# Six layers of local attention and feed-forward issued as one stream on one Trainium2 core

## The reference, cut to what matters

```python
for i in range(6):
    x = attn_layer(shift_tokens(x), Wqkv[i], q_scale[i], k_scale[i], Wo[i]) + x
    x = ffn_layer(shift_tokens(x), ln_g[i], ln_b[i], W1[i], b1[i], W2[i], b2[i]) + x
# attn_layer: 16 heads of 64; q and k divided by their norms, scaled, rotated;
#   a softmax over a band of 33 keys; the heads' outputs times Wo
# ffn_layer: layer norm, xn @ W1 + b1 split in a and gate (341 each),
#   a * gelu(gate) @ W2 + b2
```

## Time and profile before, and how to read it

| | |
|---|---|
| median of three executions | 4304.59 us (4303.39 to 4310.63) |
| the profiled execution: its own time | 4307.25 us |
| its span, first to last instruction | 4305.4 us |
| mean granted TensorE clock | 0.974 of full speed |
| PE busy / PEld busy | 94% / 74% of the span |
| DVE / ACT / POOL busy | 84% / 71% / 70% |

### The profile page before, as it was taken

The page is one execution under the profiler, slowest core; times in us unless marked ns, Lnnn a source line. Parts: engine busy times, 40 slices in busy tenths (PEclk is TensorE's granted clock), DMA queues, the critical chain, the costliest instruction groups (busy, mean ns, idle before and its releaser), DMA issues.

```text
span 4305.4 us, 111689 instructions
## 1 busy us (share of the span) xinstructions
PE 4041.0 (94%) x30864; PEld 3177.6 (74%) x30864; DVE 3601.2 (84%) x12077; ACT 3057.7 (71%) x11197; POOL 3010.0 (70%) x3393
## 2 busy tenths in 40 slices
PE   7888887899998999989999999999899999999998
PEld 5777776688876888767888768887578886688875
DVE  5676665899978999968999789999699997899985
ACT  1455544788864888838888658888388885588883
POOL 2333332799965999928999659999299995699980
PEclk9999998999999999999999999999999999999998
DMA  4222221000000000000000000000000000000000
GB/s 146 80 79 79 79 85 56 6 0 0 0 21 7 1 0 0 0 21 7 0 0 0 21 7 1 0 0 0 26 1 0 0 0 21 7 0 0 0 0 20
DMA packets 75916, 82.96 MB, mean 19 GB/s; under 512 B 13622, under 2 KB 69396, under 8 KB 74836
## 3 DMA queue, kind: packets, MB, share of 16 engines
q1 hardware_dynamic: 75732, 80.87, 5.8%
HBM read 45.33 MB, written 35.52 MB: 19 GB/s over the span
## 4 chain that ended last, share of the span: by engine, by line
PE 79%; DVE 9%; issue 5%; ACT 4%; POOL 2%; DMA 0%; DVEq 0%; SPq 0%; POOLq 0%; ACTq 0%; PEldq 0%
PE bank_pair L981 11%; PE bank L992 10%; PE bank L1007 9%; PE bank L1015 8%; PE bank L456 8%; PE bank L972 7%; PE bank L458 6%; PE bank L457 6%; PE bank_pair L1203 2%; PE bank_pair L560 1%; PE bank L554 1%; PE bank L536 1%; DVE uf L1351 1%; ACT p L637 1%; ACT sc L626 1%
## 5 line engine op out<-in xcount | busy, mean ns | idle before, releaser
L1064 ACT ACTIVATE p<-p,mx 128x128 f32<-128x128 f32 x3072 | 1195.9, 403 | 46.9 <-DVE mx L1115 45.7
L1152 POOL TENSOR_TENSOR rot<-own_crossed 128x512 f32<-128x512 f32 x768 | 984.7, 1282 | 29.6 <-DVE own_crossed L1090 29.6
L1162 POOL TENSOR_TENSOR p<-p,ri 128x512 f32<-128x512 f32 x768 | 801.7, 1044 | 54.8 <-DVE ri L1112 54.0
L1146 POOL TENSOR_TENSOR rot<-rot,rn 128x512 f32<-128x512 f32 x768 | 803.7, 1046 | 0.0
L1115 DVE CUSTOM_DVE_ANT_0 p<-bank_pair,band_f 128x128 f32<-128x128 f32 x3072 | 692.1, 282 | 5.6
L1064 ACT ACTIVATION_READ_ACCUMULATOR p<-p,mx 128x1 f32 x3072 | 617.3, 201 | 0.0
L1122 DVE COPY pTl<-bank 128x512 f32<-128x512 f32 x768 | 530.3, 691 | 89.2 <-PE bank L1007 83.7
L456 PE MATMUL bank<-wqkv_hi,xs_lo 128*128 128x512 f32 x1152 | 563.4, 489 | 40.5 <-POOL xs_lo L1135 21.7
L1044 ACT ACTIVATE qkT<-bank 128x512 f32<-128x512 f32 x768 | 454.2, 591 | 173.9 <-PE bank L972 173.8
L981 PE MATMUL bank_pair<-qkT 64*128 64x128 f32 x6144 | 549.4, 297 | 3.8 <-DVE mx L1115 3.1
L992 PE MATMUL bank<-pTl,v_sb 128*64 128x128 f32 x6144 | 512.0, 288 | 24.6 <-DVE zS L1097 19.9
(11 more groups left out here) (195 smaller groups left out, 7253.1 us busy)
## 6 DMA issues: line engine op xcount, KB each, us to landing
pos_scratch<-pos_sb SPq DMA_DIRECT2D x32, 1020.0 KB, 4.3
sc<-pos_scratch SPq DMA_DIRECT2D x32, 512.0 KB, 4.0
own_crossed<-in_L_ffn_Wqkv SPq DMA_DIRECT2D x6, 1536.0 KB, 6.7
ctx_sb<-in_ctx SPq DMA_DIRECT2D x32, 128.0 KB, 3.5
wo<-in_L_ffn_Wo SPq DMA_DIRECT2D x6, 512.0 KB, 7.1
mrow<-in_mask_BxS_fk SPq DMA_DIRECT2D x1, 2048.0 KB, 7.7
x_all<-in_x SPq DMA_DIRECT2D x4, 512.0 KB, 8.7
out<-res SPq DMA_DIRECT2D x8, 256.0 KB, 2.3
```

The costliest lines, as they stand in the source:

```text
L1064: last = nc.scalar.activation(p[:, j, h, :], p[:, j, h, :], ACT.Exp, bias=mx[:, j, h:h + 1], scale=-1.0, accum_out=psums[:, j, h:h + 1])
L1146: nc.gpsimd.tensor_tensor(rot[:, j4, :, :], rot[:, j4, :, :], rn[:, jr, (k - 4) % 2, :].unsqueeze(2).to_broadcast([128, 2 * G, DL]), ALU.m ...
L1152: nc.gpsimd.tensor_tensor(rot[:, j4, :, :], own[:, j4, :, :], crossed[:, j4, :, :], ALU.add).then_inc(L["rot0"], 1)
L1162: nc.gpsimd.tensor_tensor(p[:, j, :, :], p[:, j, :, :], ri[:, j, :].unsqueeze(2).to_broadcast([128, G, T]), ALU.mult).then_inc(L["pn"], 1)
```

## The change: one stream over six layers

The four engines' attention and feed-forward functions are replaced by one function each (`stream_tensor`, `stream_scalar`, `stream_vector`, `stream_pool`), run by `stream`. Its body is sixteen iterations, four batches; in body q of a layer the units of quad q enter, and the feed-forward of quad q - 2 is put between them, piece by piece at the iterations `at.ffn(k)`. The bodies of all layers follow one another: the feed-forward of a layer's last two quads lies beside the attention of the next layer's first two. The skew of attention grows from 11 to 16 iterations, and the order of the pieces in an iteration is new. In detail:

- Feed-forward products all go through the bank of V (`ffn_ps = v_ps`, one bank); each of them, and each V, waits until the one before it in that bank has been copied or used.
- The mean is taken out by one product with `centre_w` (identity minus mean); the mean square comes by a product with `mean_w` on all 128 partitions at once. The root is exp(-0.5 ln), on ACT. The product with the root goes to POOL, with gain on ACT before it and the offset on ACT after it (twice: as float32 and rounded); the low part is POOL's.
- Gates: DVE copies them out of PSUM with the bias (`keep_gate`, three a quad, new); gelu then works in SBUF. Values are as before.
- ACT loads the gelu tables at iteration 9 and the Ln and Exp tables again at iteration 10: two loads a quad.
- Wqkv of the next layer is split in the first iterations of body 0 of that layer, six groups of 512 columns, each right after its old content has been used last; the high part by ACT, the low part by POOL. Its raw form has a buffer of its own. W1 is split by POOL at iteration 14 of body 1; biases, gains and rotary tables are renewed by small copies on ACT and DVE. SP waits for each weight by itself.

```diff
+        def stream(eng, emit):
+            def body(l, q):
+                for k in range(BODY):
+                    emit(l, q, k)
+            body(0, 0)
+            body(0, 1)
+            with eng.Fori(0, LAYERS - 1) as l:
+                with eng.Fori(2, QUADS) as q:
+                    body(l, q)
+                body(l + 1, 0)
+                body(l + 1, 1)
+            with eng.Fori(2, QUADS) as q:
+                body(LAYERS - 1, q)
+            body(LAYERS - 1, QUADS)
+            body(LAYERS - 1, QUADS + 1)
...
+            def next_layer(l):
+                wait_apart(sp, L["wqkv_split"], l * WEIGHT_GROUPS)
+                load_wqkv(l)
+                wait_apart(sp, L["tab"], l)
+                load_scales(l)
+                wait_apart(sp, Fm["w1_split"], l)
+                load_w1(l)
+                wait_apart(sp, Fm["gain"], l)
+                wait_apart(sp, Fm["bias"], l)
+                load_vecs(l)
+                wait_apart(sp, L["WO"], l * B)
+                load_wo(l)
+                wait_apart(sp, Fm["y_mm"], l * QUADS)
+                load_w2(l)
+            return first_attention, first_ffn, next_layer
...
+        def stream_tensor(pe):
+            SHARED_AHEAD_OF_FFN = {2: ("xcg", 1, 1), 6: ("rstd", 1, 1), 8: ("gate", 3, 2), 10: ("gate", 3, 3), 12: ("u", 3, 2), 14: ("u", 3, 3)}
+            SHARED_AHEAD_OF_V = {1: ("xcg", 1, 1), 3: ("rstd", 1, 1), 7: ("gate", 3, 2), 9: ("gate", 3, 3), 11: ("u", 3, 2), 13: ("u", 3, 3)}
...
+                def v_gone():
...
+                        pe.wait_ge(L["v"], at.P + (k - 8) // 2)
...
+                        pe.wait_ge(L["z"], QUADS + at.F)
...
+                        gone, each, done = SHARED_AHEAD_OF_FFN[k]
...
+                def gate(c):
...
+                def value(c):
...
+                if on(10):
...
                     last.then_inc(L["S"], 1)
+                if at.ffn(14):
...
+                    pe.wait_ge(Fm["w2_in"], 32 * (at.lf + 1))
+                    pe.wait_ge(Fm["u"], 3 * at.F + 3)
...
+                    last.then_inc(Fm["y_mm"], 1)
                 if on(9):
...
+                    last.then_inc(L["T1"], 1)
+                if at.ffn(6):
...
+                    pe.wait_ge(Fm["w1_split"], at.lf + 1)
+                    pe.wait_ge(Fm["xn"], at.F + 1)
+                    gate(0)
+                if at.ffn(10):
...
+                    value(0)
+                if on(15):
...
                     last.then_inc(L["PV"], 1)
+                if on(9) and k % 2 == 1:
+                    if at.ffn(15):
+                        pe.wait_ge(L["z"], QUADS + at.F + 1)
+                    elif at.ffn(1, 3, 7, 9, 11, 13):
+                        gone, each, done = SHARED_AHEAD_OF_V[k]
...
+                    if at.renew() and k in (9, 11):
+                        pe.wait_ge(L["wqkv_split"], l * WEIGHT_GROUPS + UB + (k - 9) // 2 + 1)
...
+                    split_product(v_ps[:, :], [x[:, (k - 9) // UB % 4, :] for x in xs], [w[:, 2, g * G * DL:(g + 2) * G * DL] for w in wqkv]).then_inc(L["proj"], 1)
+                if at.ffn(12):
...
+                    value(2)
+                if on(4):
...
+                    if at.renew() and 0 <= k - 4 < UB:
+                        pe.wait_ge(L["wqkv_split"], l * WEIGHT_GROUPS + (k - 4) + 1)
...
+                                  [w[:, 0:2, g * G * DL:(g + 1) * G * DL] for w in wqkv]).then_inc(L["proj_qk"], 1)
+                if at.ffn(6):
+                    pe.wait_ge(Fm["gate"], 3 * at.F + 1)
+                    gate(1)
+                if at.ffn(8):
...
+                    gate(2)
+                if on(13):
...
                     last.then_inc(L["T2"], 1)
+                if at.ffn(0):
...
+                    nc.tensor.matmul(ffn_ps.rearrange("p (a n) -> p a n", a=QUAD), centre_w[:, :], shifted(at.ffn_batch(), QUAD), start=True, stop=True).then_inc(Fm["centre"], 1)
+                if at.ffn(2):
...
+                    pe.wait_ge(Fm["xsq"], at.F + 1)
+                    nc.tensor.matmul(ffn_ps[:, :], mean_w[:, :], xsq[:, :], start=True, stop=True).then_inc(Fm["var"], 1)
+                if at.ffn(10):
+                    pe.wait_ge(Fm["u"], 3 * at.F + 1)
+                    value(1)
+                if on(15) and (k - 15) % UB == UB - 1:
...
                     last.then_inc(L["WO"], 1)
...
+        def stream_scalar(act):
+            def use_table(which):
+                act.add_instruction(mybir.InstLoadActFuncSet(act_func_set_id=which, name=nc.get_next_instruction_name(), engine=mybir.EngineType.Activation))
...
+                def gelu(c):
...
+                    nc.scalar.activation(gel[0:m, c, :], gel[0:m, c, :], ACT.Gelu).then_inc(Fm["gelu"], 1)
+                def round_group(e):
...
+                if on(9):
...
+                    nc.scalar.activation(qkT[:, (k - 9) % 2, :, :].rearrange("p c n -> p (c n)"), qkT_ps[:, :], ACT.Copy).then_inc(L["qkT"], 1)
+                if on(15):
...
+                    nc.scalar.activation(oT[:, (k - 15) % 8, :], oT_ps, ACT.Copy).then_inc(L["oT"], 1)
+                if at.ffn(10):
+                    gelu(1)
+                    gelu(2)
+                    use_table(LOG_EXP_SET)
+                if on(7) and k % 2 == 1:
...
                     nc.scalar.activation(ss_log[:, j, :, :], ssc[:, j, :, :], ACT.Ln, scale=ROOT_GAIN ** 2).then_inc(L["ss_log"], 1)
...
+                    nc.scalar.activation(rn[:, (k - 7) // 2 % 4, :, :], ss_log[:, j, :, :], ACT.Exp, scale=-0.5).then_inc(L["rn"], 1)
+                if on(9) and k % 2 == 1:
...
+                    nc.scalar.activation(v_sb[:, (k - 9) % 8:(k - 9) % 8 + 2, :, :].rearrange("p u h n -> p (u h n)"), v_ps[:, :], ACT.Copy).then_inc(L["v"], 1)
+                if at.renew() and k in (5, 7):
+                    round_group(UB + (k - 5) // 2)
+                if on(10):
...
                         last = nc.scalar.activation(p[:, j, h, :], p[:, j, h, :], ACT.Exp, bias=mx[:, j, h:h + 1], scale=-1.0, accum_out=psums[:, j, h:h + 1])
...
+                if at.ffn(0):
+                    act.wait_ge(Fm["centre"], at.F + 1)
...
+                    nc.scalar.activation(xsq[:, :], ffn_ps[:, :], ACT.Square).then_inc(Fm["xsq"], 1)
+                    nc.scalar.activation(xcg[:, :], ffn_ps[:, :], ACT.Copy, scale=gain[:, 0:1]).then_inc(Fm["xcg"], 1)
+                if at.ffn(2):
...
+                    nc.scalar.activation(rstd[:, :], ffn_ps[:, :], ACT.Ln, bias=eps_col[:, 0:1], scale=1.0).then_inc(Fm["log"], 1)
...
+                    nc.scalar.activation(rstd[:, :], rstd[:, :], ACT.Exp, scale=-0.5).then_inc(Fm["rstd"], 1)
+                if at.ffn(4):
...
+                    nc.scalar.activation(xn_f[:, :], xg[:, :], ACT.Identity, bias=gain[:, 1:2], scale=1.0)
+                    nc.scalar.activation(xn_hi[:, :], xg[:, :], ACT.Identity, bias=gain[:, 1:2], scale=1.0).then_inc(Fm["xn_f"], 1)
+                if at.layer_start(1) and k == 5:
...
+                if at.ffn(9):
+                    use_table(GELU_SET)
+                    gelu(0)
+                if on(4):
...
+                    nc.scalar.activation(sq[:, k % 2, :, :].rearrange("p h n -> p (h n)"), banks[k % 2][:, :], ACT.Square).then_inc(L["square"], 1)
+                if at.renew() and k < UB:
...
+                    round_group(k)
+                if on(2) and k % UB == 2:
...
+            use_table(LOG_EXP_SET)
...
+        def stream_vector(dve):
...
+                def keep_gate(c):
...
+                    dve.wait_ge(Fm["g"], 3 * at.F + c + 1)
+                    nc.vector.tensor_scalar(gel[0:m, c, :], ffn_ps[0:m, :], b1c[0:m, 1, c:c + 1], None, ALU.add).then_inc(Fm["gate"], 1)
+                def value(c):
...
+                    dve.wait_ge(Fm["gelu"], 3 * at.F + c + 1)
+                    dve.wait_ge(Fm["a"], 3 * at.F + c + 1)
+                    nc.vector.scalar_tensor_tensor(uf[0:m, c, :], ffn_ps[0:m, :], b1c[0:m, 0, c:c + 1], gel[0:m, c, :], ALU.add, ALU.mult).then_inc(Fm["u"], 1)
+                if at.ffn(6):
...
+                    keep_gate(0)
+                if on(16) and (k - 16) % UB == UB - 1:
...
+                if at.ffn(7):
+                    keep_gate(1)
+                if at.ffn(11):
+                    value(1)
+                if on(10):
...
+                    last.then_inc(L["mx"], 1)
+                if at.ffn(10):
+                    value(0)
+                if at.layer_start(0) and k == 5:
...
+                if on(5):
...
                                             rot_x[:, :, :].rearrange("p h (s n) -> p h s n", s=2), ALU.mult).then_inc(L["own_crossed"], 1)
+                if at.ffn(12):
+                    value(2)
+                if on(5):
...
+                if at.ffn(8):
+                    keep_gate(2)
+                if at.ffn(14):
...
+                        last = nc.vector.scalar_tensor_tensor(kept, ffn_ps[rows, :].rearrange("p (a n) -> p a n", a=QUAD), b2c[rows, :], kept, ALU.add, ALU.add)
```

(32 more changed lines are left out.)

749 lines of the change are left out of this document (275 added, 474 removed).

## The result

The changed kernel takes 4423.28 us (median of four, 4416.65 to 4426.72) against 4305.15 for the kernel before (4303.39 to 4310.63): ratio 1.027, 95% interval 1.0253 to 1.0288. The forecast was 4218 us, the range ended at 4340; both are wrong, and so is the sign.

What follows compares the result with a forecast made beforehand. PE was taken to bound the kernel at 3.79 us a unit. A gain of 213.6 us less 42 (given back once), 60 (bank and bursts) and 25 (layer starts) left 86.6 us, giving 4218 us; range 4125 to 4340.

Steps and rivals of the forecast that it cites:

- the part on PE: TensorE per quad: 8.5 us of new feed-forward work, no added switch gap; body 69.1 us, gain 213.6 us in six layers.
- The sum of 3.84 against a measured 3.79: TensorE slots in attention: bare iteration 3.10 us, averaging 3.84 with V and WO, called close to the measured 3.79.
- Feed-forward work 8.5 us a quad: New TensorE work per quad: six products 4.2, centring 0.86, mean square 0.86, output 2.58 us.
- Shared bank and bursts: Waits in V's bank and bursts on DVE and ACT: 1.3 us a quad, bounds 0 and 3.8, 60 us lost.
- rival A: All covered: bursts and layer starts vanish in the skew; 4133 us, chance 0.20.
- rival B: Code is fetched again at each loop turn, 2.7 us a body, 124 us in all; 4342 us, chance 0.14.
- B's bound of 87 us: Refetching code at loop turns was to decide the sign from 87 / 46 = 1.9 us a body.
- Weights at a layer's start: POOL falls behind making low parts in body 0: 5 us, bounds 0 and 9.5, at five starts, 25 us lost.
- The 42 us given back once: Stream still fills and drains once, 26.6 us, and the last quad runs alone, 15 us beyond its PE work.
- the table loads: ACT's two loads a quad: 1.28 us each, against the skill's 2.66 us a switch with drain.
- Rival C: A table switch drains ACT in iterations 9 and 10: twice 1.9 us a quad, 175 us; 4393 us, chance 0.06.
- Rival D: Feed-forward makes gaps as in-order DVE passes late gates on: 3 us a quad, 78 more; 4296 us, chance 0.10.

## Why the prediction was wrong

**The step that failed** is in the part on PE: "The switch gap of 0.17 us is there between groups of attention already, so I add none. A body costs 16 x 3.786 + 8.5 = 69.1 us". It took the average unit of the old order for the new one. That gap isn't one price per group: it depends on which piece stands next to which, and the diff rearranged them. A body without loop turns is 16 x 3.16 + 8 x 0.70 (V) + 4 x 1.79 (WO, with T2 at 0.56 ahead of it) = 63.3 us of attention, where the forecast had 60.6. The earlier trace rows had the sign of it: its T2 slot of 0.57 stands between a product and WO, and was taken for a bare iteration too, where it is 0.39. The sum of 3.84 against a measured 3.79 was passed over as close; the bare iteration was 2.95, not 3.10. Two more terms failed beside it, the turns of the loops and the start of a layer.

**The sum, term by term**, from 4218 to 4423, a difference of 205 us:

- Feed-forward work 8.5 us a quad: right, 71.9 - 63.3 = 8.6.
- Shared bank and bursts, 1.3 us a quad: the steady body did have 1.3 to 1.4 us of such waits, in centring and V, but they came from VectorE's idle time at the turn. Without turns the slots show none; on this term rival A was right. Order and bursts together: 71.9 against 70.4, 46 times 1.5, 69 us.
- Code at loop turns, nothing in the forecast: 78 us, from the kernel without loops. This was rival B's mechanism at rival B's place, and it decides nearly as much as B's bound of 87 us asked, but it came in two forms: 1.4 us a body in 25 bodies and 2.6 in five, and 5.3 to 7.4 us at each of four turns of the outer loop, where TensorE itself stood 3.8 to 5.65 us and then had the lower clock for a while. I had looked at VectorE and ScalarE only. The Trainium skill (Advanced Engine Details and Errata, "ISA Cache") gives the engines other than TensorE two lines of 256 instructions, from which I took that a longer body is fetched again each time. The traces don't bear that out: the same body showed 0.1, 2.6 and 4.8 us, so length alone doesn't set it.
- Weights at a layer's start, 25 us: under-sized. First bodies take 86.8 against 71.9, 15 us at five starts, 75. I had POOL's wait for the first high part, 5.2 us in the trace, but not that every following low part waits again, 2.6 and 2.4 us, since its high part comes at the end of the same iteration; the place of the low parts was 30 us of it. Nor had I that TensorE's waits, 8 to 9 us by now, would bring the lower clock behind them, nor that the renewal of the rotary tables, put at under 1 us, would take 1.7 to 2.6 us beside a busy POOL, and 7.67 in one instruction with the low parts later. How the rest divides among these stays open.
- These three misses are 69 + 78 + 50 = 197 of 205 us. The 42 us given back once weren't tested by themselves.

**Right** were the table loads: 97 of 1283 ns with 1.8 us of idle time ahead of all. Rival C falls, and with it here the drain of 1.38 us that the Trainium skill (ScalarE: Activation LUTs, "What ACT_TABLE_LOAD costs") adds; taking all 96 away gave 22 us where that alone would be 132 (an estimate, 96 x 1.38). Right too was that TensorE's own work, not another engine's load, bounds the body: without loops TensorE shows no idle time from 2115 to 2190 us, a whole steady body, and no other engine is busy for over 81% of the span. Rival D isn't what happened: without loop turns no slot of a feed-forward product is longer than its neighbours make it.

The mechanism of the gain exists. With the pieces in an order whose bare slots cost as little as the old one's, the copies in the same order, the low parts later and no loop turns, the stream takes 4235 us. That this is 17 above the forecast doesn't save the forecast's sum, which was for the kernel without these changes. The change as made gives that away through its order, ScalarE's copies with it (74 us of bodies: 71.9 to 70.3), its turns (78) and its layer starts (32, first bodies 78.8 on average instead of 86.8 and the rest 1.6 less).

## What to carry to other kernels

Where TensorE is full, cost the order of its pieces, not only the pieces: read the slot from start to start for each pair of neighbours, and take a pair that no trace shows as unknown in both directions. When pieces change places on one engine, its consumers should copy in the same order, or a moved slot can turn into a wait. A loop body that grows needs its turns looked at on every engine, the bottleneck first. And where the bottleneck engine stands, read the granted clock behind the wait too: the wait isn't all that it costs.

## What was not expected of the hardware

- Four float32 transposes take 0.39, 0.56, 0.59 or 0.76 us and a product of three passes 0.57, 0.70 or 0.90, by what stands before and behind them.
- The idle time at the turn of one and the same body was 0.1, 2.6 or 4.8 us in different builds, and 40 empty instructions ahead of it, run once, made a kernel 15 us faster.
- Code without any loop, 48 bodies in a row, ran at an even 71.7 to 72.1 us in all steady bodies.
- One and the same VectorE instruction, 0.68 us in the kernel before, took 1.53 us in the changed kernel and 7.67 us in others, where it ended each time 0.55 us after a gap-free run of GpSimd.
